# A two-layer GNN and mixture-of-experts kernel: the second router reads unnormalised rows, gamma moves into the weights, and the aggregate is cut into other pieces

## The reference, cut to what matters

```python
x = x + L0_gnn(layernorm(x))                 # attention over edges
x = x + L0_moe(layernorm(x))                 # 8 experts, two per row
x = x + L1_gnn(layernorm(x))                 # below
x = x + L1_moe(layernorm(x))                 # 6 experts, one per row: below

def L1_gnn(x):                               # W is 512 x 512
    h = x * rsqrt(clip(out_degree, 1))[:, None]
    agg = segment_sum(h[src], dst)
    h = (agg * rsqrt(clip(in_degree, 1))[:, None]) @ W + b
    h = (h - mean(h)) * rsqrt(var(h) + 1e-5) * gamma + beta
    return gelu(h)

def L1_moe(x):
    probs = softmax(x @ w_gating)            # the best of 6 experts, gate1 / (gate1 + gate2 + 1e-9)
    xn = layernorm(x) * gamma                # a second norm, eps 1e-5, inside the expert
    return gate * (gelu(xn @ w1[expert]) @ w2[expert])
```

## Time and profile before

| what | value |
|---|---|
| time, median of 3 runs | 919.34 us (917.92 to 919.55) |
| the profiled execution: its time, and its span | 919.1 us, 917.4 us |
| PE busy | 836.3 us, 91% of the span |
| DVE busy | 573.5 us, 63% |
| ACT busy | 370.6 us, 40% |
| POOL busy | 222.4 us, 24% |
| mean granted TensorE clock | 0.967 |

### The profile page before, as it was taken

How to read it: one execution, slowest core, us unless ns; L and a number is a source line. 1 busy time by engine, 2 the same in 40 slices (tenths; PEclk the granted TensorE clock), 3 DMA queues, 4 the chain that set the end, 5 groups by cost and what they waited for, 6 DMA issues and landing times.

```text
span 917.4 us, 16005 instructions
## 1 busy us (share of the span) xinstructions
PE 836.3 (91%) x5066; PEld 563.9 (61%) x5066; DVE 573.5 (63%) x1888; ACT 370.6 (40%) x676; POOL 222.4 (24%) x425
## 2 busy tenths in 40 slices
PE   6999999999999999999998799999739999973996
PEld 3456555457777777777777567777414444862674
DVE  6489999257778788878776455555434419674111
ACT  1334444466665556666655333434200021331331
POOL 4100000000022102201213411222156404773443
PEclk9999999999999999999999999999969999975999
DMA  9818878695112231111834545554133540354550
GB/s 257 312 28 212 201 201 213 143 316 162 29 35 68 56 106 52 51 29 52 276 99 136 191 127 179 161 157 150 59 84 89 143 149 1 121 179 109 152 175 28
DMA packets 86980, 121.27 MB, mean 132 GB/s; under 512 B 40269, under 2 KB 49645, under 8 KB 86637
## 3 DMA queue, kind: packets, MB, share of 16 engines
q1 hardware_dynamic: 73293, 102.08, 37.9%
q0 software_dynamic: 13600, 18.11, 6.8%
HBM read 65.78 MB, written 57.08 MB: 134 GB/s over the span
## 4 chain that ended last, share of the span: by engine, by line
PE 72%; DVE 13%; issue 4%; POOL 4%; DMA 3%; ACT 2%; DVEq 0%; SPq 0%; POOLq 0%; ACTq 0%
PE ps L756 17%; PE ps L646 10%; PE ps L675 10%; PE ps L845 8%; PE ps L657 8%; PE ps L536 4%; DVE R_B L1627 4%; PE ps L763 4%; PE ps L541 3%; PE ps L870 3%; DVE R_B L1626 2%; DVE R_A L1728 1%; PE ps L486 1%; DMA R_A<-slots_d,slot 1%; PE ps L712 1%
## 5 line engine op out<-in xcount | busy, mean ns | idle before, releaser
L756 PE MATMUL ps<-R_B,R_A 128*128 x612 | 185.9, 445 | 3.0 <-ACT R_A L1252 1.1
L756 PEld LDWEIGHTS ps<-R_B,R_A 128*128 128x128 f32 x612 | 111.5, 193 | 35.1 <-issue 25.1
L1095 ACT ACTIVATE R_A<-R_A,neg_max 125x1250 f32<-125x1250 f32 x80 | 106.6, 1333 | 56.4 <-DVE neg_max L1728 54.8
L1728 DVE CUSTOM_DVE_ANT_0 R_A<-ps,R_B,neg_max 125x417 f32<-125x417 f32 (+1 forms) x160 | 97.7, 649 | 29.0 <-PE ps L646 29.0
L646 PE MATMUL ps<-R_B 64*125 64x417 f32 (+1 forms) x480 | 106.4, 544 | 1.5 <-ACT XN L1037 1.5
L675 PEld LDWEIGHTS ps<-R_W,XN 125*64 125x64 f32 x1600 | 85.3, 136 | 23.9 <-issue 23.8
L657 PE MATMUL ps<-ident,R_A 125*125 125x125 f32 x800 | 98.7, 278 | 0.0
L657 PEld LDWEIGHTS ps<-ident,R_A 125*125 125x125 f32 x800 | 94.9, 188 | 1.6 <-DVE R_W L1735 0.7
L675 PE MATMUL ps<-R_W,XN 125*64 125x125 f32 x1600 | 94.7, 272 | 0.8 <-DVE counted L1785 0.8
L1102 ACT ACTIVATE R_W<-ps 125x500 f32<-125x500 f32 x120 | 66.1, 585 | 50.5 <-PE ps L657 50.2
L1627 DVE TENSOR_SCALAR R_B<-R_B 125x418 bf16<-125x418 uint16 x200 | 77.1, 386 | 0.0
(11 more groups left out here) (278 smaller groups left out, 1134.7 us busy)
## 6 DMA issues: line engine op xcount, KB each, us to landing
slots_d<-R_B SPq DMA_DIRECT2D x9, 2322.0 KB, 12.1
R_B<-in_L_ffn_w_dram SPq DMA_DIRECT2D x28, 512.0 KB, 6.5
R_A<-slots_d SPq DMA_DIRECT2D x27, 256.0 KB
slots_d<-R_A SPq DMA_DIRECT2D x27, 256.0 KB, 2.4
counts_d<-R_A SPq DMA_DIRECT2D x10, 546.9 KB
logs_d<-R_B SPq DMA_DIRECT2D x10, 546.9 KB
R_B<-logs_d SPq DMA_DIRECT2D x10, 546.9 KB
R_B<-counts_d SPq DMA_DIRECT2D x10, 546.9 KB
```

What stands on the lines that cost most here:

```text
L756: ins = pe.matmul(bank(b, TM, width), lhs[:, c * TM:c * TM + TM], flat[:, bass.ds(e * (n * width) + c * width, width)], start=c == 0, stop ...
L1095: act.activation(SC[u % 2][h], SC[u % 2][h], ACT.Exp, bias=neg_max[:, 2 * (u % 2) + h:2 * (u % 2) + h + 1], scale=-1.0, accum_out=den[:, 2 ...
L1728: dve.tensor_tensor_reduce(SC[u % 2][h][:, a:z], bank(2 * h + g % 2, P, z - a), LNB[i % 2][:, a:z], -1.0, least if t else 3.0e38, ALU.add, ...
```

## The change

1. The first pass of the aggregate does six node tiles (pieces of 500 and 250 nodes) in the eight banks. The rest is two pieces of 250, their eight parts spread between the projections. The projections use banks 2 and 3 in turn instead of banks 4 to 7.
2. The router's turn reads X itself, as soon as `add_layer` is done, without mean and root. The gate has the mean of its columns over the 512 features subtracted (column sums on PE, one operation on DVE), and the logits' differences are multiplied by the root of the first norm at the end, for all tiles at once.
3. `unit_rows` writes the doubly normed row directly into `scaled` (now in R_W and R_B, not XN). `unit_rms` and `scaled_rows` are gone. Gamma is loaded as a column (128 x 4) and ACT multiplies W1 with it, four operations of 1536 columns, behind the moves of the first pass.
4. POOL issues the gathers of three tiles ahead of the first root. SP loads the last count rows after the gathers of tile 4, W1 after the last row is added, the gate during the first MoE layer, and stores X after `add_layer`. The row numbers are written before the layer.
5. There are four HG buffers instead of three, and the lists of PE, ACT, POOL and DVE have a new order.

```diff
+AHEAD = 3
-PIECES = ((0, 512), (512, 1024), (1024, N))
+AGGREGATED = ((0, 4), (4, 6), (6, 8), (8, 10))
+AT_ONCE = 2
...
# SP
+                    sp.dma_start(gate_w[:, :, 0:E1], L1_ffn_w_gating.rearrange("(c p) n -> p c n", c=C))\
+                      .then_inc(S("gate_in"), 16)
...
+            sp.wait_ge(rows_in[4], 16 * K0)
+            move(CS_C, counts_d[2 * C * P:N, :].rearrange("(i p) d -> p i d", p=P), S("counts_in2"))
             sp.wait_ge(rows_in[T - 1], 16 * K0)
-            move(CS_C, counts_d[2 * C * P:N, :].rearrange("(i p) d -> p i d", p=P), S("counts_in2"))
             for v, dest in ((L1_gnn_b, BIAS), (L1_gnn_gamma, GAMMA), (L1_gnn_beta, BETA)):
                 sp.dma_start(dest, v.partition_broadcast(128)).then_inc(S("vec_in"), 16)
-            sp.wait_ge(S("agg_made"), 1)
+            sp.dma_start(GAM1, L1_ffn_gamma.rearrange("(c p) -> p c", c=C), allow_slow_non_contiguous=True).then_inc(S("gam_in"), 16)
+            sp.wait_ge(S("rows_added"), K0 * T)
             for e in range(E1):
                 sp.dma_start(W1B[:, e, :].rearrange("p (c n) -> p c n", c=C),
                              L1_ffn_w1[e].rearrange("(c p) n -> p c n", c=C)).then_inc(S("w1b_in"), 16)
...
# PE
+            pe.wait_ge(S("gate_in"), 32)
+            for c in range(C):
+                ins = pe.matmul(bank(2, 128, E1), ones[:, :], gate_w[:, c, 0:E1], start=c == 0, stop=c == C - 1)
+            ins.then_inc(S("gate_sums"), 1)
...
+            def aggregate_rest(n, c):
+                g = C * n + c
+                pe.wait_ge(S("agt_moved"), g + 1 if g < 2 else C * AT_ONCE + g - 1)
                 for i in range(T):
-                    ins = aggregate(i, c, PIECES[2], c)
+                    ins = aggregate(i, c, AT_ONCE + n, g % 2)
...
+            aggregate_rest(0, 0)
+            aggregate_rest(0, 1)
             project(0)
+            aggregate_rest(0, 2)
+            aggregate_rest(0, 3)
             project(1)
             project(2)
+            aggregate_rest(1, 0)
             project(3)
             project(4)
+            aggregate_rest(1, 1)
             project(5)
+            aggregate_rest(1, 2)
             project(6)
+            aggregate_rest(1, 3)
             project(7)
-            aggregate_rest(0)
-            aggregate_rest(1)
-            aggregate_rest(2)
-            aggregate_rest(3)
             turn_unit(0)
             turn_unit(1)
+            project(8)
             route_unit(0)
-            project(8)
             turn_unit(2)
             route_unit(1)
+            rank_unit(0)
+            route_unit(2)
+            rank_unit(1)
             turn_unit(3)
+            project(9)
+            rank_unit(2)
+            route_unit(3)
...
# ACT
+            def weights_by_gamma():
+                act.wait_ge(S("gam_in"), 32)
+                act.wait_ge(S("w1b_in"), 16 * E1)
+                for c in range(C):
+                    part = W1B[:, :, H1 * c:H1 * c + H1]
+                    act.activation(part, part, ACT.Copy, scale=GAM1[:, c:c + 1]).then_inc(S("xg_made"), 1)
+            def unit_rows(i):
+                act.wait_ge(S("ln_rstd"), 3 * T + i + 1)
+                act.activation(scaled[i][:, 0:D], X[:, i, :], ACT.Identity, bias=shift[0:P, i:i + 1],
+                               scale=rstd[0:P, i:i + 1]).then_inc(S("xg_made"), 1)
+            weights_by_gamma()
+            move_rest(0, 0)
+            move_rest(0, 1)
             hidden_gelu(0)
+            move_rest(0, 2)
+            unit_rows(0)
...
# POOL
+            for i in range(AHEAD):
+                gather_rows(i)
+            row_root(0)
+            for i in range(AHEAD, T):
+                row_root(i - AHEAD + 1)
+                gather_rows(i)
+            for i in range(T - AHEAD + 1, T):
+                row_root(i)
...
-            def unit_rms(j):
...
+            def logit_roots():
+                link(pool.tensor_scalar(out_max[:, :], mv[0:P, :, 1], 1.0, LN_EPS, ALU.mult, ALU.add))
+                pool.tensor_tensor(out_max[:, :], out_max[:, :], half_pow[0:P, :], ALU.pow).then_inc(S("ln_rstd"), 1)
...
             scatter_unit(5)
+            unit_root(9)
+            logit_roots()
             scatter_unit(6)
...
# DVE
+            dve.wait_ge(S("gate_sums"), 1)
+            dve.scalar_tensor_tensor(gate_w[:, :, 0:E1], bank(2, 128, E1).unsqueeze(1).to_broadcast([128, C, E1]),
+                                     -1.0 / D, gate_w[:, :, 0:E1], ALU.mult, ALU.add).then_inc(S("gate_step"), 1)
...
-            def scaled_rows(j):
...
# DVE's new order, around the end of the layer
+            shift_rows(7)
+            add_layer(7)
+            add_bias(8)
             take_logits1(0)
             best_of(0)
             index_of(0)
             number_of(0)
+            mask_of(0)
             hidden_stats(8)
             take_logits1(1)
...
+            layer_stats(8)
+            take_slots(2)
             add_bias(9)
+            take_logits1(3)
```

More of the change, by code:

```diff
@@ L172, in gnn_moe_kernel @@
                 for n in range(K0 * T)]
-        XN_flat = XN[:, :, :].rearrange("p i d -> p (i d)")
-        scaled = [XN_flat[:, WIDE * i:WIDE * i + WIDE] for i in range(T - 1)] + [R_B[0:P, 8192:8192 + WIDE]]
+        scaled = [R_W[0:P, WIDE * i:WIDE * i + WIDE] for i in range(7)] +\
+                 [R_B[0:P, 20224 + WIDE * k:20224 + WIDE * k + WIDE] for k in range(3)]
         count_rows = [R_B[0:P, 14308 + N * k:14308 + N * k + N] for k in range(5)]
@@ L189, in gnn_moe_kernel @@
         inv_in = sb("inv_in", [P, T])
[L190 removed]
+        out_max = sb("out_max", [P, T])
         neg_max = sb("neg_max", [P, 4])
@@ L1181, in move_aggregate @@
             def move_aggregate(n, c):
-                a, z = PIECES[n]
+                a, z = (P * i for i in AGGREGATED[n])
                 act.wait_ge(S("agg_made"), C * n + c + 1)
@@ L1191, in hidden_gelu @@
                 act.wait_ge(S("hg_shift"), j + 1)
-                act.activation(HG[j % 3], HG[j % 3], ACT.Gelu).then_inc(S("hg_gelu"), 1)
-            for n in range(2):
+                act.activation(HG[j % 4], HG[j % 4], ACT.Gelu).then_inc(S("hg_gelu"), 1)
+            def weights_by_gamma():
[4 more added lines that the diff above has]
+                    act.activation(part, part, ACT.Copy, scale=GAM1[:, c:c + 1]).then_inc(S("xg_made"), 1)
@@ L1194, in _, with move_rest @@
+            def move_rest(n, c):
+                move_aggregate(AT_ONCE + n, c)
+            for n in range(AT_ONCE):
                 for c in range(C):
                     move_aggregate(n, c)
-            def unit_rows(i):
-                act.wait_ge(S("ln_rstd"), 3 * T + i + 1)
-                act.activation(XM[i], X[:, i, :], ACT.Identity, bias=shift[0:P, i:i + 1], scale=rstd[0:P, i:i + 1])\
-                   .then_inc(S("xn_made"), 1)
-            def move_unit(i):
-                act.wait_ge(S("xt_turned"), 2 * T + i + 1)
-                act.activation(XT[:, :, i * P:i * P + P],
-                               bank(i % 2, 128, C * P).rearrange("p (c n) -> p c n", c=C), ACT.Copy)\
-                   .then_inc(S("xt_moved"), 1)
@@ L1219, in _ @@
-            unit_rows(2)
-            move_rest(0)
-            move_rest(1)
-            hidden_gelu(5)
-            move_rest(2)
-            hidden_gelu(6)
             unit_rows(3)
             unit_rows(4)
-            move_rest(3)
+            move_rest(1, 1)
+            hidden_gelu(5)
+            move_rest(1, 2)
+            unit_rows(5)
+            hidden_gelu(6)
+            move_rest(1, 3)
+            unit_rows(6)
             move_unit(0)
+            move_unit(1)
             hidden_gelu(7)
-            move_unit(1)
@@ L1390, in _, with gather_rows @@
             pool.wait_ge(S("y_made"), MT0)
-            for i in range(T + 2):
-                if i > 1:
-                    n = i - 2
-                    rstd_tile(S("ln_stat"), 2 * T + n + 1, n, inv_out[:, n:n + 1], S("ln_rstd"))
-                for k in range(K0 if i < T else 0):
+            def gather_rows(i):
+                for k in range(K0):
                     pool.indirect_dma_start(rows[K0 * i + k], None, slots0_d,
@@ L2136, in _ @@
-            centre_rows(4)
-            add_bias(6)
             hidden_stats(5)
-            shift_rows(4)
-            layer_stats(2)
-            hidden_stats(6)
-            add_layer(4)
             centre_rows(5)
             shift_rows(5)
+            add_layer(5)
+            layer_stats(5)
+            add_bias(6)
+            hidden_stats(6)
+            centre_rows(6)
+            shift_rows(6)
+            add_layer(6)
+            layer_stats(6)
             add_bias(7)
-            layer_stats(3)
@@ L2163, in _ @@
             index_of(0)
             number_of(0)
-            add_bias(8)
+            mask_of(0)
             hidden_stats(8)
             take_logits1(1)
-            add_layer(7)
-            mask_of(0)
-            centre_rows(8)
             best_of(1)
+            index_of(1)
```

(29 more changed lines are left out.)

286 lines of the change are left out of this document (114 added, 172 removed).

## The result

The changed kernel takes 923.75 us (median of 16 runs, 921.79 to 925.33) against 919.39 us of the kernel before (16 runs, 917.92 to 920.96). The ratio is 1.0040, 95% interval 1.0032 to 1.0049. It is slower by 4.4 us, where 2.2 us less were forecast, and it lies above the range. The profiled execution took 924.66 us for a span of 922.9 us.

The account below looks back on a forecast made before the run. PE was taken to bound the kernel until `project(7)` and the aggregate end, then a tail: 796.8 + 36.0 = 832.8 instead of 835.0 us, 2.2 us earlier. 919.1 - 2.2 + 0.2 = 917.1 us, range 913.5 to 921.9 us.

Parts of the forecast that it names:

- The bound and the split into first turn and tail: PE alone bounds up to the first turn, forecast 3.4 us later; from there to the last scatter's issue, 5.2 us shorter.
- The speed of the first pass: Aggregate's first pass: 5.06 us of PE per source tile instead of 6.90, rows coming two tiles every 11.35 us.
- The count rows: Last count rows, 1.2 MB, loaded beside tile 5's gathers: delay between 0 and 4 us, taken as 1 us.
- rival (b): First pass: gathers slip 3 to 4 us behind the count rows and the gain is gone; 919.5 us, chance 0.13.
- The tail: First turn to the end of the last scatter's issue: 36.0 us instead of 41.2, so 5.2 us shorter.
- the ends of 33.4 and 37.7 us: Bounds for first turn to last scatter: POOL's list gives 33.4 us, half clock in the second half 37.7 us.
- Rival (c), the clock ahead of `project(9)`: After the first turn, the clock falls before `project(9)`, costing it up to 3 us; tail 41 us, 922.1 us, chance 0.16.
- Its sign: What would decide for the clock's fall before `project(9)`: granted clock leaves 1.00 less than 10 us behind Z, PE's finish of `project(7)`.
- Gamma in the weights: ACT's four multiplications of W1, 6.4 us, done at 745.4 us, 2.0 us before PE needs the following move; costed at nothing.
- The landing: Last scatter's issue to the expert loop: 5.86 us in flight, later work unchanged, so no extra time forecast.
- The starting line of the sum: Forecast times were counted on from the earlier kernel's one profiled execution, 919.1 us, with the first gather at 666.31 us.

Follow-up runs that it names:

- e_ahead4: The changed kernel with the gathers of four tiles, not three, issued ahead of the first root; 0.9950 of the kernel before.
- e_counts_first: The changed kernel with the last count rows loaded ahead of all gathers instead of behind those of tile 4; 0.9982 of the kernel before.
- b_counts_early: The kernel before with one part of the change alone, the last count rows loaded behind the gathers of tile 4; 1.0002 of the kernel before.
- e_eight: The changed kernel with eight node tiles in the first pass instead of six, the rest's four parts between the projections; 0.9954 of the kernel before.
- e_ahead3b: The changed kernel with each gather behind the root three tiles back on POOL, not two; 0.9976 of the kernel before.
- e_roots_last: The changed kernel with the two operations for the logits' roots behind POOL's last scatter, not ahead of tile 6's; 1.0014 of the kernel before.
- e_ahead4_roots: The changed kernel with four tiles of gathers ahead of the first root and the logits' roots behind the last scatter; 0.9945 of the kernel before.

## Why the prediction was wrong, by its steps

- **The bound and the split into first turn and tail: right.** Both terms moved, and they carry the result.
- **The speed of the first pass: right.** 5.08 us a source tile in e_ahead4 (5.06 forecast). Where nothing disturbed them, two tiles of rows came every 10.9 to 11.2 us (e_counts_first, tiles 3, 5, 7 and 9 at 688.70, 699.78, 710.71 and 721.87 us; 11.35 forecast from the earlier trace rows). With the count rows out of the way the first turn is at 129.8 us; the forecast without its 1 us for them is 796.8 - 1 - 666.31 = 129.5 us.
- **The count rows: the step that failed.** "The gathers move little, so I take 1 us", with 4 us as the upper end. Measured: 10.39 instead of 5.5 us for the gather, and 6.2 us of first pass. The kind of bound was right, its size and the choice in it were wrong. The load's packets took the DMA engines for 5 us (696 to 701 us, q1 at 91.6%; alone, in the kernel before, they also took 5 us, 725 to 730 us), and the gather came 4.9 us late, by the whole of it and not by a quarter. And a delay of PE was priced as the wait alone; behind it came 5 us at half clock. That a load can hold up a gather was seen in rival (b), which was given 0.13 and only 3 to 4 us (its own numbers give 919.8, not 919.5 us). Compared with the forecast's 69.2 us from first gather to the end of the first pass, 74.8 were measured. Of the 5.6 us more, 2.5 are the clock behind the wait, 1.0 the waits (4.8 against 3.8 us), 1.0 the clock of the first tiles (0.64 over 8 us, 2.9 us lost where 1.9 were taken), 0.6 PE's start, and 0.5 is left over.
- **The tail: right in size** (35.4 against 36.0 us), in part by luck. The logits' roots cost 2.2 instead of under 1.5 us, and that does not matter. Between the ends of 33.4 and 37.7 us the tail goes with the clock: the seven tails above run from 35.2 to 37.5 us, and 36.0 was a pick between the ends. The upper end has the tail's second half at half clock: before, that is the stretch behind 812 us, at 0.51.
- **Rival (c), the clock ahead of `project(9)`: the fall is real, its price was not.** Its sign came true: the clock left 1.00 less than 10 us behind the first turn (9.6 us in the changed kernel, 804.50 to 814.1 us). That costs the projection 1.0 to 2.5 us over 3.6 us in the seven versions (`project(8)` takes 3.60 us at full clock; up to 3 us were feared), and the tail did not become 41 us, 5 us more than forecast, but 35.2 to 37.5 us: the clock is back at 1.00 within the projection, behind 3.2 to 6.9 us at 0.50, and stays there for 6.5 to 10 us.
- **Gamma in the weights: right.** The loads land at 745.4 us and the four multiplications take 5.97 us (6.4 estimated), done at 751.4 us; `move_rest(0, 0)` follows, and `aggregate_rest(0, 2)`, itself late, starts without a gap at 755.2 us. In e_ahead4, where PE is not late, there is no gap either. The strided gamma column landed in 4.8 us and held up nothing. ACT in order of time, after:

```profile
745.43 5.97 ACT L1214 ACTIVATE R_B<-R_B 128x1536 f32<-128x1536 f32 x4 [1.57 <-DMA R_B<-in_L_ffn_w_dram]
```

- **The landing was costed at nothing** and is 0.7 us longer in the changed kernel, whose last scatters leave back to back.
- **The starting line of the sum** was a single profile; the changed kernel's began 2.2 us later, which the medians bear out only in part.

The forecast's sign was wrong by one term of 1 us that measured 6.2: without that load the changed kernel is faster (0.9982), as forecast (0.9976). That the two ratios lie so close is partly luck: in the profile of e_counts_first the first turn is where the sum puts it, but the tail is 1.5 us and the landing 1.3 us longer than forecast.

## What to carry to other kernels

When a change takes work from an engine that just covered a row of transfers, the slack goes first: compare the new time of a step with the rate at which its input comes, and then look at everything else that the change puts on the same DMA engines. A bulk load beside gathers that wait for one another delayed them here by about its own length, 5 us. It cost nothing where PE had slack (b_counts_early, e_eight) or the gathers a longer lead (e_ahead4, e_ahead3b), and 6 us where neither was so. A wait of TensorE cost more than its length here: behind 4.70 us came 5 us at half clock, behind 0.35 and 0.81 us nothing. One more tile of lead on the gathers brought the first turn 9 us forward here, moving the load 6 us.

## What the runs showed of the hardware that was not expected

A gather of 125 rows of 2 KB takes about 5.5 us without the load and 8.5 to 12.3 us beside a load of 1.2 MB on another queue (all eleven profiles that have the two together). How it is held up depends on what is in flight when the load starts. In the changed kernel, e_eight and e_roots_last no gather was moving: the load's packets went first, and the gathers' began only when it was nearly through (in the changed kernel 5 us behind the issue, and 1.5 us for the gather issued at 684.00 us, with nothing beside it). In e_ahead4, e_ahead3b, e_ahead4_roots and b_counts_early gathers were moving, and both queues' packets mix for the whole of the load, which then takes about 10 us instead of 5 (in e_ahead4 q1 has packets from 686 to 697 us, and q0 has some in each of these microseconds). Queues in e_ahead4 from 689 to 691 us:

```profile
q1 hardware_dynamic: 66, 0.33, 84.8%
q0 software_dynamic: 25, 0.06, 17.8%
```

In the other three the load's queue alone has packets for 4 to 5 us (696 to 700 us in the changed kernel), though a gather was issued close to the load, and ahead of it in the changed kernel and in e_eight; whether that gather had no packets ready or was passed over, no run shows.

The same instructions in the same order took 4.6 to 6.1 us for `project(9)` in seven profiles, and 2.3 us of the tail go with it. A power of 125 x 10 on POOL takes 1.98 us, that of one column mostly 0.55 to 0.57 us; from these two sizes I estimate 0.16 us for each further column. Some of POOL's operations on one column took twice their time or more (1.03 and 1.06 us for the two operations of a root at 681.61 us in the changed kernel, 0.27 and 0.57 us at 686.85 us). The slow ones run beside DVE's add of a tile (L2013, from 681.85 us there; likewise at 709.62 us, where no DMA moved), the fast ones do not, and e_eight shows the same (1.03 and 1.07 us beside the add at 704.79 us). No run was made to test it. Such a root lies in the circle and adds some 1 us to it where it stands there, as at 681.61 us.

What is left open: the 2.4 us by which e_roots_last is faster in timed runs than its profile shows, and why e_ahead3b is timed some 2 us above e_ahead4.
